# One written order for SyncE too, and a ring of routed tiles handed out tile by tile, in a graph-convolution kernel

## The reference

```python
def ssp(v): return jax.nn.softplus(v) - jnp.log(2.0)

h    = x @ W_in2f
Wij  = ssp(f_ij @ W_filt1 + b_filt1) @ W_filt2 + b_filt2     # f_ij: 20 features of an edge
Wij  = Wij * rcut_ij[:, None]                                # one weight of each edge
x_ij = h[idx_j] * Wij                                        # idx_j is dst, idx_i is src
agg  = segment_sum(x_ij, idx_i, num_segments=n_atoms)
out  = ssp(agg @ W_out1 + b_out1) @ W_out2 + b_out2
x    = layernorm(x + out)
```

## Time and profile before

| what | value |
|---|---|
| median of 3 runs | 2171.71 us |
| the profiled execution, its own time | 2169.02 us |
| its span, first to last instruction | 2167.3 us |
| mean granted TensorE clock | 0.974 |
| busy: PE, PEld | 2039.4, 1713.0 us |
| busy: DVE, ACT, POOL | 1943.3, 1587.9, 1700.0 us |
| mean DMA rate | 109 GB/s |

### The profile page before, as it was taken

One profiled execution on the slowest core, in us unless ns is written; L12 is line 12 of the kernel. 1 busy time (PEld: TensorE's weight loads), 2 busy tenths in 40 slices (PEclk: granted clock), 3 DMA queues, 4 the chain that ended last, 5 costly groups with the idle time before them and its releaser, 6 DMA issues.

```text
span 2167.3 us, 52608 instructions
## 1 busy us (share of the span) xinstructions
PE 2039.4 (94%) x16433; PEld 1713.0 (79%) x16433; DVE 1943.3 (90%) x4035; ACT 1587.9 (73%) x3852; POOL 1700.0 (78%) x1038
## 2 busy tenths in 40 slices
PE   2589999999999999999999999999999999999946
PEld 2468888888888888888888888888888888888823
DVE  6669999999999999999999999999999999999847
ACT  0278777777777777777877777777778777778617
POOL 2048888888888888888888888888888888888864
PEclk8689999999999999999999999999999999999978
DMA  9546656656656656566566565665665665666584
GB/s 328 200 86 94 103 92 102 103 83 107 101 87 105 98 96 104 88 103 103 82 108 99 92 106 91 102 102 84 103 102 83 107 99 88 106 94 87 83 210 131
DMA packets 346333, 235.22 MB, mean 109 GB/s; under 512 B 86087, under 2 KB 325554, under 8 KB 345850
## 3 DMA queue, kind: packets, MB, share of 16 engines
q0 software_dynamic: 140976, 64.22, 32.1%
q1 hardware_dynamic: 194598, 150.79, 27.0%
q10 hardware_dynamic: 10476, 16.77, 2.1%
HBM read 145.44 MB, written 86.20 MB: 107 GB/s over the span
## 4 chain that ended last, share of the span: by engine, by line
PE 33%; DMA 25%; issue 15%; POOL 14%; DVE 10%; ACT 3%; DVEq 0%; ACTq 0%; POOLq 0%; SPq 0%
DMA table<-total,index 23%; POOL table L714 13%; PE unit_psum L1670 9%; PE unit_psum L1689 7%; PE both_psum L1627 6%; PE total_psum L1640 4%; PE pre_psum L1608 3%; PE both_psum L1652 2%; DVE scat_hot L1325 1%; DVE route_hot L1308 1%; DVE hidden L1246 1%; PE both_psum L1623 1%; DVE same L1226 1%; DMA b_o<-in_b_o 1%; DVE acc_t L1342 1%
## 5 line engine op out<-in xcount | busy, mean ns | idle before, releaser
L714 POOL DMA_INDIRECT table<-total,index x979 | 1641.3, 1676 | 410.5 <-issue 242.9
L1670 PE MATMUL unit_psum<-moving,route_hot 128*128 128x258 f32 x4088 | 656.9, 298 | 2.0 <-DVE acc_t L1342 1.4
L892 ACT ACTIVATE ring<-unit_psum 128x258 fp32r<-128x258 f32 x1022 | 389.5, 399 | 299.8 <-PE unit_psum L1670 280.9
L1670 PEld LDWEIGHTS unit_psum<-moving,route_hot 128*128 128x128 f32 x4088 | 534.5, 189 | 62.3 <-ACT ring L892 42.4
L1689 PE MATMUL unit_psum<-scat_hot,ring 64*128 64x448 f32 x4088 | 459.2, 371 | 10.5 <-DVE scat_hot L1325 9.5
L1325 DVE TENSOR_SCALAR scat_hot<-node_iota,ring 128x448 fp32r<-128x448 uint16 x1022 | 461.4, 465 | 0.8 <-ACT ring L892 0.7
L869 ACT ACTIVATE h_dst<-both_psum,edge_cols 128x128 f32<-128x128 f32 x1564 | 451.5, 388 | 7.3 <-DVE message L1272 2.4
L1689 PEld LDWEIGHTS unit_psum<-scat_hot,ring 64*128 64x128 f32 x4088 | 376.3, 185 | 86.3 <-ACT ring L892 37.8
L1308 DVE TENSOR_SCALAR route_hot<-node_iota,slot_cols 128x896 fp32r<-128x896 uint16 x584 | 395.1, 703 | 37.3 <-PE unit_psum L1670 37.3
L1627 PE MATMUL both_psum<-w_f,hidden 128*128 128x128 f32 x3128 | 425.7, 279 | 0.0
L1627 PEld LDWEIGHTS both_psum<-w_f,hidden 128*128 128x128 f32 x3128 | 400.5, 193 | 21.5 <-issue 16.2
(11 more groups left out here) (124 smaller groups left out, 1574.3 us busy)
## 6 DMA issues: line engine op xcount, KB each, us to landing
dst_b<-dst SPq DMA_DIRECT2D x391, 128.0 KB
src_b<-src SPq DMA_DIRECT2D x245, 128.0 KB
f_t<-in_f_t SPq DMA_DIRECT2D x98, 256.0 KB, 4.4
table<-total,index POOLq DMA_INDIRECT x979
table<-zeros ACTq DMA_DIRECT2D x20, 640.0 KB, 10.1
window<-h_parts SPq DMA_DIRECT2D x391, 32.0 KB
parts<-table SPq DMA_DIRECT2D x48, 256.0 KB, 5.0
h_parts<-h_out SPq DMA_DIRECT2D x12, 384.0 KB, 2.8
```

Source lines behind the costliest of these rows:

```text
L714: pool.indirect_dma_start(tables[k], bass.IndirectOffsetOnAxis(index[:, i, k:k + 1], 0), total[:, i, k, 0:DIM], None, compute_op=ALU.add). ...
L892: act.activation(ring[:, r[1] % RING, k, :], unit_psum[:, k % 2, 0:MOVING], ACT.Copy).then_inc(ring_done, 1)
L1670: last = pe.matmul(unit_psum[:, k % 2, 0:MOVING], route_hot[:, tile, k * P:(k + 1) * P], moving[:, tile, :], start=(tile == 0), stop=(tile ...
```

## The change

1. `unit(u)` and `rest()` of PE, DVE and ACT are written anew, in another order. The calls in a period are the same in number and kind: 67 on PE, 77 on DVE, 49 on ACT. POOL keeps its order.
2. SP gets a `unit` and a `rest` of its own. The loads are the same; several windows are now loaded in a row, and the loads of other tiles lie between them.
3. The ring has 28 tiles (`RING_TILES`, found by `place_in_ring`) for the 49 before. A tile goes back to a list of free ones as soon as it is summed, and `keep_slots` waits for `taken_done` up to the number in `FREED_BY`. The memory that this frees is left unused.
4. `scat_hot` keeps its seven buffers, but is used in turn: a one-hot waits for the seventh before it, and no more for the step before in the tail.
5. Steps and routed groups are numbered apart. Step `s` still sums one tile of the routed groups `s-6` to `s`.

```diff
-RING = SLOT_TILES
+STEPS_AT = (0, 1, 2)
+HOTS = 7
...
-        ring = at(0, "ring", [P, RING, SLOT_TILES, MOVING], F32R)
+        ring = at(0, "ring", [P, RING_TILES, MOVING], F32R)
...
+def place_in_ring():
+    free, tiles, where, freed_by, last = [], 0, {}, {}, {}
+    s = 0
+    for r in range(ROUTES):
+        for k in range(SLOT_TILES):
+            if not free:
+                free.append(tiles)
+                tiles += 1
+            where[r, k] = free.pop(0)
+            if where[r, k] in last:
+                freed_by[r, k] = last[where[r, k]]
+        while s < STEPS and NEWEST[s] == r:
+            for x in places_taken((0, s)):
+                tile = where[taken((0, s), x)[1], s % SLOT_TILES]
+                free.append(tile)
+                last[tile] = through_taken((0, s), x)
+            s += 1
+    return tiles, where, freed_by
...
# SP
+            def unit(u):
+                next_window(g(6)); next_window(g(7))
+                next_dst(g(8))
+                next_window(g(8)); next_window(g(9))
+                next_src(g(7), plain)
...
# ACT, keep_slots
-                if taken(m, 0) is not None and k == 0:
-                    act.wait_ge(taken_done, through_taken(m, 0))
+                if (r[1], k) in FREED_BY:
+                    act.wait_ge(taken_done, FREED_BY[r[1], k])
...
# DVE, slot_one_hot
-                if isinstance(m[0], int) and m[1] > ROUTES:
-                    dve.wait_ge(taken_done, through_taken(plus(m, -1), RING - 1))
-                elif taken(plus(m, -1), (x + 1) % RING) is not None:
-                    dve.wait_ge(taken_done, through_taken(plus(m, -1), (x + 1) % RING))
+                n = through_taken(s, x)
+                if n > HOTS:
+                    dve.wait_ge(taken_done, n - HOTS)
...
# DVE, unit
-                add_slice(m(1), 0); add_slice(m(1), 1)
-                slot_one_hot(m(2), 0)
+                add_slice(s(-1), 0); add_slice(s(-1), 1)
+                slot_one_hot(s(0), 0); slot_one_hot(s(0), 1)
                 multiply(g(3), plain)
...
# DVE, rest, the end of it
-                slot_one_hot((0, 151), 0); slot_one_hot((0, 151), 1); slot_one_hot((0, 151), 2)
-                add_slice((0, 151), 0); add_slice((0, 151), 1)
-                slot_one_hot((0, 152), 0); slot_one_hot((0, 152), 1)
-                add_slice((0, 152), 0); add_slice((0, 152), 1)
+                slot_one_hot((0, 148), 2); slot_one_hot((0, 148), 3); slot_one_hot((0, 149), 0)
+                slot_one_hot((0, 149), 1); slot_one_hot((0, 149), 2)
+                add_slice((0, 147), 0); add_slice((0, 147), 1)
+                slot_one_hot((0, 150), 0); slot_one_hot((0, 150), 1); slot_one_hot((0, 151), 0)
```

More of the change, by code:

```diff
@@ new lines, with taken, slot_tile, places_taken @@
+NEWEST = newest_routes()
+STEPS = len(NEWEST)
+STEP_AFTER = {n: s for s, n in enumerate(NEWEST)}
+def taken(s, x):
+    if not 0 <= s[1] < STEPS:
+        return None
+    r = step_route(s[1] - SLOT_TILES) + 1 + x
+    oldest = NEWEST[s[1] - SLOT_TILES] + 1 if s[1] >= SLOT_TILES else 0
+    return (s[0], r) if oldest <= r <= NEWEST[s[1]] else None
+def slot_tile(s):
+    return s[1] % SLOT_TILES
+def places_taken(s):
+    return [x for x in range(2 * ROUTES) if taken(s, x) is not None] if 0 <= s[1] < STEPS else []
@@ L1472, in rest @@
[L1472 to L1478 removed]
+                slot_one_hot((0, 145), 6); slot_one_hot((0, 146), 0)
@@ L1689, in sum_slots @@
                         last = pe.matmul(unit_psum[:, strip, 0:BUCKET],
-                                         ring[rows, r[1] % RING, slot_tile(m), part * DIM:(part + 1) * DIM],
-                                         scat_hot[rows, r[1] % RING, :], start=first and part == 0,
+                                         ring[rows, RING_AT[r[1], slot_tile(s)], part * DIM:(part + 1) * DIM],
+                                         scat_hot[rows, (n - 1) % HOTS, :], start=first and part == 0,
                                          stop=final and part == 1)
@@ L1781, in rest @@
[L1781 to L1783 removed]
+                route((0, 143), 2); route((0, 143), 3)
+                sum_repeated((0, 384), plain)
+                route((0, 143), 4)
+                second_layer((0, 386))
+                route((0, 143), 5); route((0, 143), 6)
+                gather((0, 388))
@@ new lines, in rest @@
+                first_layer((0, 195))
+                sum_slots((0, 143), 0); sum_slots((0, 143), 1); sum_slots((0, 143), 2); sum_slots((0, 143), 3)
+                sum_slots((0, 143), 4); sum_slots((0, 143), 5); sum_slots((0, 143), 6)
+                gather((0, 389))
+                second_layer((0, 387))
+                sum_repeated((0, 386), plain)
+                route((0, 144), 0); route((0, 144), 1)
+                second_layer((0, 388))
+                sum_repeated((0, 387), plain)
@@ new lines, in rest @@
+                gather((0, 390))
+                route((0, 144), 2); route((0, 144), 3)
+                second_layer((0, 389))
+                route((0, 144), 4); route((0, 144), 5); route((0, 144), 6)
+                sum_repeated((0, 389), plain)
+                sum_slots((0, 144), 0); sum_slots((0, 144), 1); sum_slots((0, 144), 2); sum_slots((0, 144), 3)
+                sum_slots((0, 144), 4); sum_slots((0, 144), 5); sum_slots((0, 144), 6)
+                second_layer((0, 390))
+                route((0, 145), 0); route((0, 145), 1); route((0, 145), 2); route((0, 145), 3)
```

503 lines of the change are left out of this document (243 added, 260 removed).

## The result

| | before | after |
|---|---|---|
| median of the runs, us | 2173.67 (2170.34 to 2182.67, 4) | 2208.52 (2202.97 to 2215.42, 4) |
| profiled execution, us | 2169.02 | 2210.26 |
| its span, us | 2167.3 | 2208.5 |
| period of eight groups, us | 39.67 | 40.60 |

The ratio is 1.0155, 95% interval [1.0112, 1.0199]: slower by 35 us, where 7 us faster were forecast, and outside the range. In what follows a kernel is compared by its ratio to the kernel before that ran on the same chip. The latter's median was 2165.8 to 2180.8 us in the four groups of runs, so absolute times of different groups aren't compared. A period is read from the one profiled execution of a kernel, start to start of `bias_band` matmuls; 0.1 us of it is 5 us of the time, about what single runs of a kernel differ by.

The account below looks back on a forecast made before the run. PE was taken as the bound, with POOL as a second one. Terms of -7 us (row of six and changeovers), +2 (DVE in time) and -2 (tail) gave -7 us: 2162 profiled, 2165 as a median, range 2150 to 2189.

Parts of the forecast that it names:

- POOL holds the pace: Rival: scatters on POOL set the period, so the loop gains nothing; median 2171 us, chance 0.20.
- Point 1: PE's row of six `route` gives way to at most three, so less stall on copies: -0.30 us per period.
- Point 2: More changeovers on PE between `route` and other calls: +0.15 us per period.
- Point 3: DVE finishing in time for PE's waiting matmuls at two places: +0.04 us per period, bounds 0 and +0.6.
- Place 2: Where PE's `bias_f` matmul follows DVE's two additions and `multiply(g(3))`; slack put at 0.3 us.
- The port pair: Skill's rule that two-port DVE instructions and GpSimd's descriptor writes block each other; used to explain scatters of 1.54 to 2.66 us.
- Points 4 and 5: SP's new load order, 0 (bounds 0 and +5 us); ring by tiles and `scat_hot` in turn, 0 (within 3 us).
- Point 6: In the tail, one-hots now stand ahead of the additions, shortening PE's waits at six places: -2 us, bounds 0 and -5.
- DVE comes late: Rival: PE waits 0.3 us for DVE at each of two places, 0.45 us per period; median 2192 us, chance 0.22.

Follow-up runs that it names:

- b_33: The kernel before with only its row of six `route` broken by `first_layer`, into rows of four and three: 2211.48 us, ratio 1.0214.
- a_mult7: The kernel after with `multiply(g(7))` on DVE moved ahead of two `compare_dst` and a `make_index`: 2198.39 us, ratio 1.0132 to the kernel before.
- a_oldsp: The kernel after with SP's loads in the old order: 2208.23 us, ratio 1.0175 to the kernel before.
- b_hots: The kernel before with only `scat_hot` used in turn, waiting for the sum seven before: 2180.72 us, ratio 0.9999.

## Why the prediction was wrong

- **What bounds the kernel before.** Both bounds were named. The runs speak for POOL's pace, 0.26 us per period above PE's own 39.41. So while its scatters kept their mean of 1.68 us, no order of PE's could gain in the loop, and the old order of PE had 12 us to gain from POOL alone. The rival "POOL holds the pace" was the better reading of the earlier trace rows.
- **Point 1, the row of six (-0.30).** This step failed. Without scatters the row went from 3.59 us for 3.11 packed (3.01 in my sum, which left out that a `route` ahead of a `first_layer` costs 0.1 more), 0.48 of stall, to a row of three with 0.31 and a pair after a `sum_repeated` with 0.19: 0.50. I had taken it that two calls and a `gather` are just what the copy needs. That holds only if ACT is free: at 1028.69 the copy stood behind a `weigh_h_dst`, while another pair behind a `sum_repeated`, at 1038.79, takes 1.08 us. The stall only moved. And b_33 shows that part of it was cover for DVE.
- **Point 2, changeovers (+0.15).** Right: 0.19 in all less the 0.02 of point 1 is 0.17.
- **Point 3, DVE in time (+0.04, bounds 0 to +0.6).** The step that failed by most. I looked at two places, took DVE's instructions at their length before, and let DVE catch up with its 2.3 us of idle time, which lies elsewhere in the period. Place 2 has 0.16 us of slack where I had 0.3, and loses 0.04 us. PE waits at a third, the last multiply of a period, with next to no slack and 0.57 us of delay by the scatters ahead of it. The loss beyond PE's own order is 1.00 - 0.26 = 0.74 us per period, and the one wait is 0.42 us, of which a_mult7 won 0.37 back. The rest is the small pieces of 0.07 to 0.16 us, which go away with the scatters. Why each falls where it does was not tried one by one.
- **The port pair.** The Trainium skill's rule ("SBUF — State Buffer", "Who interferes with whom") was weighed on POOL's side alone. Mean scatters went only from 1.680 to 1.691 us. It is DVE's side that paid: 463 to 488 ns against 446 undisturbed. By the rule tensor_scalar can be blocked, for the whole instruction of the other engine; tensor_tensor with both inputs in SBUF meets GpSimd's reads only, and that descriptors need the write side is called inferred there. The runs agree on the forms. On the length they don't: a one-hot inside a scatter of 1.5 us or more lost 0.35 us at the most, so if it is that lock, POOL holds it for a part of the scatter only. That it is the lock was not shown.
- **Points 4 and 5 (0).** Right as far as they were tried, by a_oldsp and b_hots; the ring by tiles alone was not.
- **Point 6, the tail (-2).** The sums gained 3.2 us. But more of the routing now comes after the last pair of groups, and from there to the last sum it is 46.5 us for 44.3.
- **The rival "DVE comes late"** had the right kind and sign at a chance of 0.22. It had other places, and its 0.45 us per period was half of the measured 0.93, and so the range ended 20 us short.

## What to carry to other kernels

A nearly full engine's slack isn't its idle time over a period but what is left in one run between two of its idle gaps, up to the instruction that someone waits for. Take it from start to start: durations that overlap gave one delay of 0.57 us as 0.9. When an order is rewritten, work this out for every such instruction, and with the length that it has beside the others' worst. A stall seen between two engines may be cover for a third, so break it alone before counting it as gain.

## What the hardware showed that I had not expected

- Scatters on POOL stretch tensor_scalar on DVE: 446 to 488 ns for 448 columns, and 283 to 382 ns for four, as means in the kernel after. The worst single slot one-hot took 0.77 us. The tensor_tensor kinds of 610 and 680 ns and the scalar_tensor_tensor of 1210 kept their length everywhere.
- Only part of a scatter does it. By the records of both kernels, 14% of the slot one-hots before and 21% after took over 0.475 us, and 87 and 89% of these started 0.4 to 1.15 us after a scatter had. The phase isn't all: 39 and 38% of all slot one-hots start there, and 30 and 48% of those are stretched. Equal work in another order gets another share.
- A one-hot of eight columns has a duration of 0.22 us and costs 0.13 from start to start, where one of 440 or of 448 columns costs 0.36. Cutting eight columns off saves 4 ns or less and costs 0.13 us.
- Two DVE instructions in a row can both be lengthened by a scatter while only one delay results: a `moved` of 0.59 us for 0.28 put the next start off by nothing.
- The same kernel before took 2165.8 to 2180.8 us on different chips. The profiles of before and b_hots, with a mean scatter of 1.68 and 1.70 us and periods of 39.67 and 40.00, agree with POOL setting the pace. The chips were not compared beyond that.
